# The operands of an unused wide product at the head of a loop round, in a kernel that runs an integration beside a mixture of experts

## What is computed

```python
x = x + _L0_conv_ref(_ln_c(x), ...)          # a global attention of each image
t = _to_tokens(x)
t = t + _L0_ffn_ref(_ln_t(t), ...)           # 8 experts of hidden width 512, the best 2 of each token
x = _from_tokens(t, x)
x = x + _L1_conv_ref(_ln_c(x), ...)          # a 3 x 3 convolution in 8 groups
t = _to_tokens(x)
t = t + _L1_ffn_ref(_ln_t(t), ...)           # Runge-Kutta steps of a network of tanh layers
```

```python
for e in range(E):
    h = jax.nn.gelu(xt @ W1[e] + b1[e], approximate=False)
    ye = h @ W2[e] + b2[e]
    out = out + ye * scores[:, e:e + 1]
```

## Time and profile before

| | before |
|---|---|
| median of 3 runs | 2901.73 us |
| lowest and highest | 2900.7 and 2904.1 us |
| the profiled execution: its time | 2900.79 us |
| its span in the profile | 2899.0 us |
| granted TensorE clock, mean of the span | 0.980 |
| busy: PE, PEld, DVE, ACT, POOL | 97%, 83%, 82%, 54%, 25% |
| the expert loop, 63 rounds | 213.4 to 1577.7 us of the span |

### The profile page before, as it was taken

The page is one execution under the profiler, slowest core; times in us unless marked ns, Lnnn a source line. Parts: engine busy times, 40 slices in busy tenths (PEclk is TensorE's granted clock), DMA queues, the critical chain, the costliest instruction groups (busy, mean ns, idle before and its releaser), DMA issues.

```text
span 2899.0 us, 208902 instructions
## 1 busy us (share of the span) xinstructions
PE 2813.0 (97%) x82250; PEld 2411.6 (83%) x82250; DVE 2371.2 (82%) x13418; ACT 1551.6 (54%) x10124; POOL 737.0 (25%) x1417
## 2 busy tenths in 40 slices
PE   7789999999999999999999999999999999999999
PEld 3468888888888888888888887888889999999998
DVE  4668888888888888888888887888878888888887
ACT  5445556555555555555555444444445555555555
POOL 5023323323323333233232000111112222222222
PEclk8779999999999999999999999999999999999999
DMA  3000000000000000000000000000000000000000
GB/s 117 0 8 16 11 11 14 11 11 14 11 11 14 11 12 13 11 14 11 11 14 8 1 0 1 0 0 0 0 16 0 0 0 0 0 0 0 0 0 14
DMA packets 21983, 28.21 MB, mean 10 GB/s; under 512 B 4385, under 2 KB 12897, under 8 KB 21545
## 3 DMA queue, kind: packets, MB, share of 16 engines
q1 hardware_dynamic: 21928, 27.48, 3.2%
HBM read 25.24 MB, written 2.23 MB: 9 GB/s over the span
## 4 chain that ended last, share of the span: by engine, by line
PE 92%; DVE 4%; ACT 2%; issue 1%; DMA 0%; SPq 0%; DVEq 0%; ACTq 0%; POOLq 0%; POOL 0%
PE PSUM L675 22%; PE PSUM L681 20%; PE PSUM L862 17%; PE PSUM L736 12%; PE PSUM L666 5%; PE PSUM L858 4%; PE PSUM L838 2%; PE PSUM L843 2%; DVE PSUM L1367 1%; PE PSUM L773 1%; PE PSUM L702 1%; ACT HA L1050 1%; PE PSUM L706 1%; PE PSUM L743 1%; PE PSUM L513 1%
## 5 line engine op out<-in xcount | busy, mean ns | idle before, releaser
L1367 DVE TENSOR_REDUCE PSUM<-PSUM 128x32 f32<-128x64 f32 x2912 | 623.6, 232 | 99.3 <-PE PSUM L681 52.5
L675 PEld LDWEIGHTS PSUM<-HA,RL 128*128 128x128 f16 x11648 | 396.8, 96 | 205.0 <-ACT HA L1050 194.8
L1051 ACT ACTIVATE PSUM<-PSUM 128x32 f32<-128x32 f32 x2912 | 561.0, 194 | 0.0
L1050 ACT ACTIVATE HA<-PSUM 128x32 f16<-128x32 f32 x1456 | 288.9, 199 | 467.6 <-DVE PSUM L1367 467.5
L1050 ACT ACTIVATE HB<-PSUM 128x32 f16<-128x32 f32 x1456 | 289.1, 200 | 466.9 <-DVE PSUM L1367 466.9
L675 PE MATMUL PSUM<-HA,RL 128*128 128x16 f16 x11648 | 511.8, 170 | 15.4 <-ACT HA L1050 7.6
L675 PE MATMUL PSUM<-HB,RLU 128*128 128x16 f16 x11648 | 511.2, 170 | 4.8 <-ACT HB L1050 0.2
L420 POOL TENSOR_TENSOR G<-G 128x512 f16<-128x512 f32 x256 | 296.1, 1157 | 684.6 <-ACT G L1023 684.6
L681 PE MATMUL PSUM<-HA,RH 128*128 128x32 f16 x11648 | 465.0, 177 | 0.0
L681 PE MATMUL PSUM<-HB,RHU 128*128 128x32 f16 x11648 | 464.3, 177 | 0.0
L675 PEld LDWEIGHTS PSUM<-HB,RLU 128*128 128x128 f16 x11648 | 393.5, 96 | 47.9 <-ACT HB L1050 2.4
(11 more groups left out here) (309 smaller groups left out, 6982.0 us busy)
## 6 DMA issues: line engine op xcount, KB each, us to landing
G<-scores SPq DMA_DIRECT2D x64, 256.0 KB, 3.2
N<-in_x SPq DMA_DIRECT2D x8, 256.0 KB, 4.8
NHL<-in_w SPq DMA_DIRECT2D x1, 2048.0 KB, 10.3
STF<-in_w SPq DMA_DIRECT2D x1, 2048.0 KB, 14.7
out<-W2HL SPq DMA_DIRECT2D x8, 256.0 KB, 2.4
G<-in_r SPq DMA_DIRECT2D x1, 1024.0 KB, 5.5
R1K<-in_r SPq DMA_DIRECT2D x1, 256.0 KB, 2.8
R3F<-in_r SPq DMA_DIRECT2D x1, 256.0 KB, 5.7
```

The lines of the kernel that those rows point to most:

```text
L675: mm(out[m // 2][:, 2 * B * (m % 2):2 * B * (m % 2) + B], lo[:, k, m], src[:, k, 0], start=False, stop=False)
L1050: A(hi[:, 2 * h:2 * h + 2, 0], src, ACT.Tanh, scale=1.0 / scale).then_inc(rk_hi, 1)
L1051: A(full, src, ACT.Tanh, scale=1.0 / scale).then_inc(rk_f, 1)
L1367: v.tensor_reduce(bank[:, SUM:SUM + 2 * B].rearrange("p (m b) -> p m b", m=2), bank[:, 0:4 * B].rearrange("p (m c b) -> p m b c", m=2, c=2 ...
```

## The change

The unused wide product of place 0 took fixed operands, CKH and CKL. Now it takes the operands of the round's first expert product (m = 0, k = 0): the weights W1H of the round's expert and the tokens NH of the round's tile. It stands behind the two lines that make `at[0]` and `at[1]`. Its result is still not read, and its shape and its place among the products are the same.

```diff
                 first = isinstance(g, int) and g == 0
                 if slot == 0:
-                    mm(PS[6][:, :], CKH[:, 0:128], CKL[:, 0:TILE], start=True, stop=True)
                     at[0] = (g % NE) * MC if isinstance(g, int) else pe.snap((g % NE) * MC)
                     at[1] = g // NE if isinstance(g, int) else pe.snap(g // NE)
+                    mm(PS[6][:, :], W1H.rearrange("p e m n -> p (e m) n")[:, bass.ds(at[0], 1)].squeeze(1),
+                       NH[:, bass.ts(at[1], TILE)], start=True, stop=True)
                 if slot == SLOTS // 2 and not first:
```

## The result

The changed kernel takes 2911.47 us (median of 8 runs, 2909.3 to 2913.5), the kernel before 2900.61 (median of 8, 2898.9 to 2904.1). The ratio is 1.0037, with a 95% interval of 1.0027 to 1.0046: **slower by 10.9 us**, or 10.9/63 = 0.172 us in each round of the expert loop. The forecast was 2914.5 us, slower. The profiled execution took 2911.63 us, its span is 2909.8 us, 10.8 more than before. All ratios here are of fast executions: one of the kernel before, in the first set of experiments, took 6316.6 us for a reason that isn't known, and stays out of them.

The account below looks back on a forecast made before the run. TensorE was taken as the bound, waiting for its sequencer at round heads; 0.29 us delay in place 0, less place 1's gain, averaged +0.203 us, times 63 is 12.8 us: forecast 2914.5 us, range 2907 to 2920.

Parts of the forecast that it names:

- What bounds: Expert loop: TensorE is close to the bound, and at each round's head waits 0.186 us for its own sequencer.
- The price of (4): Place 0: two register operations put between injections and wide product start that product 0.29 us later.
- part (1): Place 0: the wide product reads other operands of the same shape, so its streaming time stays: nothing.
- The gain (3): Place 1: without the two register operations the first expert product follows L681 by 0.025 instead of 0.10 us, gaining 0.075.
- the full 0.28: Cost of each round if TensorE's queue already hid place 1's address work, so that moving it gained nothing there.
- There is no slack behind the wide product of place 0: Place 0: the wide product is already the last thing L675 waits for, by 0.03 to 0.05 us.
- rival A: Place 0: injections and idle time cover the address work; under 0.075 us delay the gain outweighs; 2897.0 us; chance 0.07.
- The sum, 0.203 us a round: Head to L675 on HB: average lengthening of a round, place 1's gain included; 63 rounds make 12.8 us.
- The three kinds of round (ScalarE earlier or later against the head) average: L666 to L675 on HB: 1.92 us against 1.71, 1.74 and 1.70 gives +0.21, +0.18 and +0.22, averaging +0.203.
- B (VectorE): Behind place 1: VectorE becomes the bound and place 1's gain is lost; 17.6 us, 2919.3 us; chance 0.10.
- C (only the second operation): Place 0: the first operation runs beside the injections; delay 0.13, net 0.05 us a round, 2904.9 us; chance 0.08.

Follow-up runs that it names:

- e1: Kernel before, with the wide product reading only its tokens by a register address; the other half of the address work stays in place 1: 2901.97 us.
- e2: Kernel before, with the wide product reading only its weights by a register address; the other half of the address work stays in place 1: 2902.92 us.
- e3: The changed kernel, with quotient and remainder worked out once more ahead of the wide product, into registers that the expert products use: 2932.77 us.
- e8: e6 with the change on top: the wide product reads the round's operands by the held registers, without division or remainder ahead of it: 2904.45 us.
- e5: Kernel before, with the unused wide product of place 0 taken out: 2900.58 us.
- e4: Kernel before, wide product with fixed operands, the address work done right behind it in place 0, into registers: 2902.96 us.
- e6: Kernel before, with the next round's quotient and remainder worked out at the end of place 15 and held in registers; wide product fixed: 2895.07 us.
- e9: e6 without the wide product of place 0: 2894.79 us.
- e7: Kernel before, with fixed operands in all expert products, so no address work for them (63 of 64 rounds compute wrongly): 2893.08 us.

## Why the prediction was right, point by point

**What bounds: right.** The sequencer has no lead at the head of a round, and work ahead of the wide product came out as "issue" of its load, 0.23 us a round. I had written near 0.3; the work begins some 0.31 us before that load, and its first part runs beside the injections' own loads (606.12 to 606.23).

**The price of (4), +0.29 us: right.** Start of the address work 0.03 us behind the injections (I took 0.02), durations 153 and 57 ns (156 and 57), wide product at 0.35, L675 on HA 0.22 behind it, so the other operands cost nothing by themselves, as part (1) said. It is not only the right sum: e1, e2, e3 and e8 put other durations in the same place, and L675 on HB moved with the wide product by the same hundredths.

**The gain (3), 0.075 us: right.** The first expert product follows L681 by 0.025 us. e1 and e2 show that already half of the work moved brings all of it. Against it stood what I had drawn from the Trainium skill (TensorE: Matmul & The Clock Gate, section Architectural detail), which gives TensorE a queue of 64; that such a queue hides this work is my inference and not in the page, and by it a round would have cost the full 0.28 us. No run here shows how deep that queue is; what e1 shows is that place 1 hides 101 or 113 ns of such work and not both operations of 156 and 57.

**"There is no slack behind the wide product of place 0": the place is right, the words too strong.** e5 takes the wide product away and nothing is gained. In the kernel before, the few hundredths at L675 on HA were swallowed by the register wait of place 1. A delay at the wide product counts only from where it outweighs that wait, as rival A said with its 0.075 us: e1, delayed by 0.12, lost 0.02 us a round (and 1.999 against 1.979 us from VectorE's sum ahead of the head to L675 on HB).

**The sum, 0.203 us a round, is the term that was mis-sized.** It measured 0.175, just below the spread of 0.18 to 0.24 that I gave the step, and 63 x 0.028 = 1.8 us of the 3.0 by which the forecast was high. From L666 to L675 on HB came out at 1.92 us, exactly as said. What failed is "The three kinds of round (ScalarE earlier or later against the head) average": I subtracted the new 1.92 from three old distances, 1.71, 1.74 and 1.70, as if the head, L666, were a fixed mark in the round. It isn't: in those rounds it stood earlier or later against ScalarE. In the changed kernel ScalarE's half of HA starts 0.03 us behind the injections (606.15, 606.12), as in the round at 625.40, and there the prediction had +0.18. A mark on the engines' own chain is VectorE's L1367 ahead of the head (L1368 now); one head before and one after:

```profile
603.51 0.43 DVE L1367 TENSOR_REDUCE PSUM<-PSUM 128x32 f32<-128x64 f32 x2
```

```profile
605.88 0.43 DVE L1368 TENSOR_REDUCE PSUM<-PSUM 128x32 f32<-128x64 f32 x2
```

From there to L675 on HB are 605.49 - 603.51 = 1.98 us before, and 1.98 in the two other kinds as well (from 625.16 and from 646.81). Now they are 608.04 - 605.88 = 2.16, in this round and the next two. That is +0.18 in every kind, and the round's +0.175. Over all 62 rounds of both traces the means are 1.979 and 2.159. Measured from L666 they are 1.725 and 1.919, +0.194: so about 0.009 of the 0.028 is that the three kinds are not equally frequent (37 of the 62 rounds have 1.73 or 1.74), and 0.014 that the mark moved. Of the rest of the 3.0 us, 1.1 is the base: I added the step to the median of 2901.7 shown then, and with more runs the kernel before stands at 2900.6.

**The rivals.** A (covered) fell with the change itself. e4 gave it its best case, the work behind a wide product that needs no address, and that too covers only a part: L675 on HA was still 0.13 us late. B (VectorE) fell as the prediction said it would show: L1368 after place 1 comes 608.83 - 607.48 = 1.35 us behind the L1368 before it, not 1.44, and e3 shows no other engine taking over up to 0.27 us. C (only the second operation) fell: the sequencer begins the first one only 0.03 us behind the injections, and the delay of the wide product, 0.29 us, is more than both operations last (0.21). e8 is against the milder form of it, that division and remainder are what costs.

**Open:** why nearly all rounds of the changed kernel (59 of 62) have the head at the same distance from ScalarE, where the kernel before has three. And e6 and e9, whose medians are within 0.3 us of each other, have rounds of 21.545 and 21.565. A round is read from one execution, and the two profiled ones took 2893.42 and 2894.79 us, which is that difference (63 x 0.02 = 1.3 us). It doesn't lie at the head: from VectorE's sum ahead of it to the sum two places on there are 2.688 and 2.687 us, and every place behind is 0.0015 us shorter in e6. What sets that pace is not known. So a difference of 0.02 us between the rounds of two kernels need not come from their heads.

## What to carry to other kernels

Where an engine has just met its own sequencer (behind a loop's jump, "issue" in front of the first load), the first product that needs an address from a register pays for the register work in front of it, and everything behind that product pays with it. So an operand with a fixed address is worth keeping there, even in a product that nobody uses. Register work right behind such a product isn't free either: e4 had it there and gained nothing. Work out a round's addresses in the round before, where the sequencer is ahead of the engine, and hold them over the jump: that was worth 5.2 us here, where moving them up within the round cost 10.9. When a step's cost is a difference between two distances, take both from a mark that is on the chain which sets the time, not from the head of a loop.

## What the runs showed of the hardware that I had not expected

- A register instruction costs more than its duration. Behind the 153 ns operation there was a pause of some 0.06 us. With 0.058 us for each operation and 0.044 us off once, the delay of the wide product is 0.153 + 0.057 + 0.116 - 0.044 = 0.282 us for the change, 0.115 for e1, 0.192 for e8 and 0.556 for e3. Measured from L666 it was 0.29, 0.12, 0.20 and 0.56. The two constants are fitted to these kernels, an estimate. What doesn't rest on them: two operations in e8 (84 and 36 ns) last 19 ns more than the one of e1 (101 ns), and delayed the wide product 0.08 us more.
- What an operation lasts depends on a division or a remainder in it: 101 and 113 ns with one (e1, e2), 153 with both and some sums and products, 84 for seven copies, products and sums without either (e8), 57 for three. With both, and two of the results written into registers that are kept, one took 238 and 248 ns (e6, e4). Why that is so much more than 153 isn't shown.
- A single register operation of 32 ns with a product waiting behind it put that product 0.09 us later (place 14, e6 against e7).
- Idle time at each loop head was followed, in 3 of 62 rounds of e3, by a fall of the granted clock from 1.00 to 0.50, and each such round was 1 us longer.
- The idle time of a load can be put down to an engine that had been done for 0.19 us (e4), where the sequencer was still at its register operations.
